# A state-space recurrence in two lanes: TensorE alternates one lane's turning of the next product with the other lane's output sum

## What is computed

```python
delta = softplus(u @ W_delta + b_delta)
Bm, Cm = u @ W_B, u @ W_C
A = -exp(A_log)
def step(h, inp):
    d_t, B_t, C_t, u_t = inp
    dA = exp(d_t[..., None] * A)
    h = dA * h + d_t[..., None] * B_t[:, None, :] * u_t[..., None]
    y_t = einsum('bdn,bn->bd', h, C_t)
    return h, y_t
```

## Time and profile before

| | us |
|---|---|
| runs: median (lowest to highest) | 1390.96 (1388.8 to 1392.76) |
| the profiled execution, its own time | 1393.41 |
| its span, first to last instruction | 1391.8 |
| mean granted TensorE clock in it | 0.828 |
| PE busy | 961.7 |
| DVE busy | 868.4 |
| ACT busy | 666.6 |
| POOL busy | 254.6 |

### The profile page before, as it was taken

One profiled execution on the slowest core, in us unless ns is written; L12 is line 12 of the kernel. 1 busy time (PEld: TensorE's weight loads), 2 busy tenths in 40 slices (PEclk: granted clock), 3 DMA queues, 4 the chain that ended last, 5 costly groups with the idle time before them and its releaser, 6 DMA issues. The chain is left out here.

```text
span 1391.8 us, 12083 instructions
## 1 busy us (share of the span) xinstructions
PE 961.7 (69%) x3654; PEld 529.3 (38%) x3656; DVE 868.4 (62%) x1703; ACT 666.6 (48%) x1829; POOL 254.6 (18%) x153
## 2 busy tenths in 40 slices
PE   3533756666698968988925155666668897798984
PEld 3421333333336633444415033333333464344342
DVE  1387533333547949999726873333336595899994
ACT  1304385555043428666811337555523243667872
POOL 1011024444316010000000100344442330000000
PEclk9955867888898979999966567787779897899997
DMA  6100011111000000000010001111100000000000
GB/s 192 27 0 1 8 49 46 48 48 48 0 0 1 0 1 0 1 1 1 0 44 0 1 0 34 46 45 46 48 28 0 1 1 0 0 1 1 0 1 16
DMA packets 26814, 27.41 MB, mean 20 GB/s; under 512 B 7172, under 2 KB 17146, under 8 KB 26746
## 3 DMA queue, kind: packets, MB, share of 16 engines
q1 hardware_dynamic: 24776, 24.63, 6.1%
q10 hardware_dynamic: 1970, 1.97, 0.5%
HBM read 25.28 MB, written 1.31 MB: 19 GB/s over the span
## 5 line engine op out<-in xcount | busy, mean ns | idle before, releaser
L1301 DVE TENSOR_TENSOR_SCAN mem<-mem,ps 128x1024 f32<-128x1024 f32 x64 | 142.9, 2274 | 222.6 <-PE ps L722 222.6
L728 PE MATMUL ps<-mem,ident 128*128 128x512 f32 x256 | 183.2, 882 | 124.0 <-POOL mem L1503 124.0
L1488 POOL TENSOR_TENSOR rs<-ve,minus_half 128x4 f32<-128x4 f32 (+2 forms) x60 | 102.1, 1709 | 827.2 <-DVE ve L1118 698.9
L876 PE MATMUL ps<-mem,ident 128*128 128x512 f32 x512 | 231.4, 600 | 30.6 <-DVE mem L1456 29.8
L908 ACT ACTIVATE mem<-ps 77x512 f32<-77x512 f32 (+7 forms) x172 | 103.6, 605 | 250.9 <-PE ps L817 69.5
L1078 ACT ACTIVATE mem<-mem 128x32 f32<-128x32 f32 x1024 | 217.8, 309 | 0.0
L1503 POOL TENSOR_TENSOR mem<-mem 128x1024 f32<-128x1024 f32 x64 | 148.9, 2348 | 293.3 <-DVE mem L1301 293.3
L1456 DVE SCALAR_TENSOR_TENSOR mem<-mem 128x1024 f32<-128x1024 f32 x128 | 159.4, 1282 | 13.3 <-ACT mem L1078 9.5
L876 PEld LDWEIGHTS ps<-mem,ident 128*128 128x128 f32 x512 | 94.0, 190 | 167.0 <-issue 92.7
L728 PEld LDWEIGHTS ps<-mem,ident 128*128 128x128 f32 x256 | 70.4, 288 | 216.9 <-POOL mem L1503 149.0
L994 ACT ACTIVATE mem<-mem,m_A 128x511 f32<-128x511 f32 x128 | 84.8, 712 | 141.6 <-DVE mem L1301 140.7
(11 more groups left out here) (219 smaller groups left out, 1232.3 us busy)
## 6 DMA issues: line engine op xcount, KB each, us to landing
mem<-bc_rows SPq DMA_DIRECT2D x64, 256.0 KB, 3.1
x<-in_x_dram SPq DMA_DIRECT2D x4, 256.0 KB, 3.6
out_dram<-x SPq DMA_DIRECT2D x4, 256.0 KB, 2.3
mask<-in_mask_BxSxS_ik_dram SPq DMA_DIRECT2D x4, 154.0 KB, 3.2
mem<-n_L_ffn_expert_down_dram SPq DMA_DIRECT2D x1, 512.0 KB
mem<-in_L_xattn_Wo_dram SPq DMA_DIRECT2D x1, 512.0 KB
mem<-in_L_xattn_Wv_dram ACTq DMA_DIRECT2D x1, 512.0 KB
a_q<-in_L_xattn_Wq_dram SPq DMA_DIRECT2D x1, 512.0 KB, 4.8
```

The lines of the kernel that those rows point to most:

```text
L728: mm = pe.matmul(ps[:, j, :], ident[:], HC[s][:, n % 2, j, :], start=(n == 0), stop=(n == NS - 1), skip_group_check=True)
L876: mm = pe.matmul(ps[:, j, :], ident[:], WH[s][:, h % WB, j * 512:(j + 1) * 512], start=(h == 0), stop=(h == PH - 1), skip_group_check=True)
L1301: nc.vector.tensor_tensor_scan((HS, TU)[n % 2][s][:].rearrange(flat), dA[s][:, n % 2].rearrange(flat), dbu.rearrange(flat), 0.0, ALU.mult, ...
L1488: nc.gpsimd.tensor_tensor(RS[s][0:rows, i * n:(i + 1) * n], VE[s][0:rows, i * n:(i + 1) * n], minus_half[0:rows, 0:n], ALU.pow)\
```

## The change

Two numbers in PE's program and the place of the output sum. The turning keeps 3.7 + n for lane 0 and gets 4.0 + n for lane 1. The sum of round n is issued one turn of the generator later, after the same lane's turning of round n+1, with the numbers 5.2 + n (lane 0) and 5.8 + n (lane 1) in place of 4.5 + n. The last sum of a lane has a turn of its own, and the product with W_out moves from 21 to 22. What each piece waits for and what it computes stay the same, as do the programs of all other engines.

```diff
-                    for n in range(NS):
-                        if s in BLEND_LANES:
-                            yield 3.7 + n
+                    for n in range(NS + 1):
+                        if n < NS and s in BLEND_LANES:
+                            yield (3.7, 4.0)[s] + n
                             w.next(G("dz_ready", s))
                             if n == 0:
                                 w.next(G("xT_ready", s))
...
                             mm.then_inc(G("dbu_done", s), 1)
-                        yield 4.5 + n
-                        w.next(G("hc_done", s))
-                        for j in range(DJ):
-                            mm = pe.matmul(ps[:, j, :], ident[:], HC[s][:, n % 2, j, :],
-                                           start=(n == 0), stop=(n == NS - 1), skip_group_check=True)
-                        mm.then_inc(G("y_acc", s), 1)
-                    yield 5 + NS
+                        if n >= 1:
+                            yield (4.2, 4.8)[s] + n
+                            w.next(G("hc_done", s))
+                            for j in range(DJ):
+                                mm = pe.matmul(ps[:, j, :], ident[:], HC[s][:, (n - 1) % 2, j, :],
+                                               start=(n == 1), stop=(n == NS), skip_group_check=True)
+                            mm.then_inc(G("y_acc", s), 1)
+                    yield 6 + NS
                     w.next(G("yg_ready", s))
```

## The result

| | before | changed |
|---|---|---|
| median of the runs, us | 1391.03 | 1207.4 |
| lowest to highest | 1388.8 to 1392.76 | 1207.17 to 1210.36 |
| the profiled execution | 1393.41 | 1207.17 |
| its span | 1391.8 | 1205.5 |
| mean granted TensorE clock | 0.828 | 0.858 |

The median of before is the mean of its two middle runs; the 1390.96 in the earlier table is the lower of the two. The ratio of the times is 0.869, with a 95% interval of 0.867 to 0.870. The change takes 186.3 us off the span; the forecast was 176.4.

The account below looks back on a forecast made before the run. The bound was taken to be a circle in PE's issue order, turnings behind sums waiting for POOL; opened, ACT bounds at 5.64 us a round. Saving 88.1 + 88.3 = 176.4 gave 1393.4 - 176.4 = 1217.0 us, range 1209 to 1250.

Parts of the forecast that it names:

- The circle through POOL: Recurrence: next turning stands behind two sums that wait for POOL's products; round 10.89 us, and the change removes that wait.
- The round of 5.64 us: Recurrence with the change: ACT's work, 189.39 to 195.03 without waits, bounds each round, against 11.41 us before.
- PE's 5.3 us with 0.06 lost from a turning to a sum: PE's work per round at the upper clock: 5.17 us plus 0.06 per change from turning to sum, under ACT's 5.64.
- The time in hand: One round placed in time: ACT has 3.9 and 2.4 us to spare for the scans, so it never waits.
- The worry about writes to a lane's own PSUM beside its scan: Sums might stretch scans of their own lane; taken as nothing, but scans twice as long would give 1316 us.
- The sum over the loops: Both recurrence passes: first loop 93.4 us long, saving 88.1 and 88.3 us, together 176.4.
- Nothing changes outside the loops: Start and stages behind the recurrence: no saving or loss entered the sum, 1393.4 - 176.4 = 1217.0 us.
- The alternating clock: Recurrence: PE still granted 0.80, its work becomes 6.6 us a round and bounds it; 1246 us, chance 0.10.
- The lower level throughout: Recurrence: TensorE at its lower clock all the time, 10.3 us a round; 1359 us, chance 0.03.
- the shown loads: Recurrence: lower clock, plus a 0.34 us weight load at each of four changes, 11.7 us a round; 1401 us, chance 0.02.
- the stretched engines: Recurrence: engines slowed by running beside more others, scans of 3.0 us giving 1229, far end 1316 us; chance 0.06.
- the forecast's second rival: Recurrence: TensorE at its lower clock throughout, as if transposes pulled it down, 10.3 us a round; 1359 us, chance 0.03.

Follow-up runs that it names:

- the plain deferral: Against the changed kernel: both sums still issued one round late, but not alternated (turning 0, turning 1, sum 0, sum 1); 1206.53 us.
- lane 1 alone: Against the changed kernel: only lane 1's sum is issued a round late, lane 0's stays in its own round; 1299.27 us.
- three products ahead of it: Kernel before, with three unused 128x1024 products on DVE behind each loop, ahead of the next stages; 1387.51 us.

## Why the prediction was right and where it was wrong

The measured 1207.4 us lies 1.6 us under the range, whose low end was 1209.

1. *The circle through POOL, and that it opens.* Right: no wait for POOL is left on PE, and the run with lane 0 left undeferred brings it back.
2. *The round of 5.64 us, with ACT as the bound.* Right to the last digit. Half of the sum away changes nothing, a quarter of one lane's DZ away shortens the round to 5.25.
3. *PE's 5.3 us with 0.06 lost from a turning to a sum.* Turning 0 at 236.84 is followed by the sum at 237.77, which is 0.93 against eight steps of 0.11, so 0.05 lost; from turning 1 at 239.49 to 240.36 nothing is. PE's own round is 5.25.
4. *The time in hand.* Never used up: ACT waits nowhere in the loop. The worry about writes to a lane's own PSUM beside its scan does not arise with this order, as the placed round itself shows: each scan has the other lane's sum beside it. Scans are 2285 ns on average, against 2274 before. In the plain deferral the sums do run beside their own lane's scans, and the scans take 2274. Taking nothing for it was right.
5. *The sum over the loops.* 93.4 us was forecast for the first and 93.5 measured; 176.4 saved in both, 176.1 measured.
6. *Nothing changes outside the loops.* This is the step that failed. The sum was 1393.4 - 176.4: the stages outside the loops entered it at nothing. The only room for them was the 8 us from 1217.0 down to 1209, for "a better clock in the stages behind and for the spread of the runs", and no row gave that size. The runs showed some 10 us there: 8.1 from cross-attention, 1.8 from the start and 0.3 from all else. The execution from which the sum was made explains little of it, as it was only 2.4 us above the median; from the median the forecast was 1214.6. Cross-attention stood at its long end in it, 147.7 us in both passes, and the same work takes 142.7 to 147.8 across the kernels, by where the clock falls. With 10 us for the two passes and 4 for the start the low end would have been 1217.0 - 14 = 1203. Nothing in the trace of before told whether these stages would get shorter. That they did in both passes was luck: in the plain deferral the second pass stayed at 147.8.
7. *The rivals.* The alternating clock did not come: 1.00 in the loop. The transposes ran at the upper level, 1.04 for eight, mixed with the sums. The lower level throughout, the shown loads and the stretched engines did not come either. What the forecast credited without testing is the alternation: I let it stand as the way in which PE is filled, and the plain deferral does as well.
8. *An expectation that failed too*: lane 1 alone, 1264 forecast and 1299 measured. The round was 7.67 us for the 7.5 expected where the clock stayed up, but in half of the rounds it fell, and they took 9.34.

## What to carry to other kernels

When two lanes share an in-order engine, look for the circle in the order of issue: an instruction that waits for a slow helper and stands ahead of one that the next round's chain needs. Issue the helper's consumer a round later, if the buffers allow; here the time of a round then became the work of the busiest engine, and adding it up from pitches in the trace gave it to 0.01 us. Name a term for the stages that the change does not touch: where their clock alternates, the same instructions took 142.7 to 147.8 us here, in different kernels and even in two passes of one execution (144.0 and 147.8), and a forecast from one profile carries that in full.

## What the runs showed of the hardware

The clock's fall is not fixed by the length of a pause alone. In the kernel with lane 1 deferred a pause of 2.21 us is followed by the lower level in one round (a sum of 2.87) and by the upper in the next (1.98). Cross-attention kept its clock behind a pause of 1.24 us, but behind pauses of 1.88 us in the plain deferral it was back with the second product in one pass and stayed low for some 10 us in the other. So a stage that begins later can end earlier: in the kernel before, cross-attention of the first pass ran from 380.94 to 528.63 us, and with three products ahead of it from 383.50 to 526.72.

The Trainium skill, "TensorE: Matmul & The Clock Gate", Part 4 (PE-mode transpose), has the upper level not engage for transposes. In the loop of the changed kernel they run at 0.11 us each at a granted clock of 1.00, and where half of the sums is left out, so that 16 transposes stand beside 4 records of the sums in a round, the clock still averages 0.89. By that rule the forecast's second rival would have come, with 1359 us; the trace does not agree, at least for transposes of f32 data mixed with other matmuls. A loop of transposes alone was not tried.
